# An attention and spiking-FFN kernel whose weighted sums, side work and transposes are put in other slots

## The reference

```
xn = layernorm(x)
q = einsum('bnhd,hed->bnhe', xn.reshape(B, N, 16, 16), Wq)
attn = softmax(einsum('bnhe,bmhe->bhnm', q, q) * 4)
s = einsum('bhnm,bmhe->bnhe', attn, q).reshape(B, N, D) @ Wp.T + bp
h = square(relu(xn @ W_fc.T))          # 1024 hidden
y = h @ W_proj.T
spikes = five steps: mem = 0.9*mem + y - reset; count mem > 1
out = x + s * silu(count / 5)
```

## Time and profile before

| what | value |
|---|---|
| median of 3 runs | 2579.01 us (2578.52 to 2580.41) |
| profiled execution, its own time | 2580.22 us |
| span of the profiled execution | 2578.3 us |
| mean granted TensorE clock | 0.991 of full speed |
| PE, ACT, DVE, POOL busy | 94%, 77%, 61%, 29% |

### The profile page before, as it was taken

How to read it: one execution, slowest core, us unless ns; L and a number is a source line. 1 busy time by engine, 2 the same in 40 slices (tenths; PEclk the granted TensorE clock), 3 DMA queues, 4 the chain that set the end, 5 groups by cost and what they waited for, 6 DMA issues and landing times.

```text
span 2578.3 us, 63759 instructions
## 1 busy us (share of the span) xinstructions
PE 2419.0 (94%) x23484; PEld 920.8 (36%) x23484; DVE 1567.1 (61%) x2581; ACT 1983.1 (77%) x2121; POOL 737.4 (29%) x681
## 2 busy tenths in 40 slices
PE   4999999999999999999999999999999999999997
PEld 2333333333333333333333333333333333333333
DVE  6456555766556675555765556665556755557664
ACT  2778778787777878778787787877778787787775
POOL 5123222333222332222332223332223332223420
PEclk7999999999999999999999999999999999999998
DMA  3011030210302102030110302102021120301200
GB/s 123 26 43 58 18 100 18 59 54 13 94 18 74 44 26 76 18 100 19 43 59 18 100 18 63 55 14 89 18 78 40 31 72 18 100 18 46 73 18 27
DMA packets 61487, 127.36 MB, mean 49 GB/s; under 512 B 15873, under 2 KB 17154, under 8 KB 58754
## 3 DMA queue, kind: packets, MB, share of 16 engines
q1 hardware_dynamic: 61186, 123.25, 15.5%
HBM read 89.11 MB, written 34.08 MB: 48 GB/s over the span
## 4 chain that ended last, share of the span: by engine, by line
PE 71%; ACT 14%; DVE 8%; issue 4%; SPq 1%; ACTq 0%; DMA 0%; DVEq 0%; POOL 0%; POOLq 0%
PE acc L624 34%; PE scores L650 18%; ACT e L804 14%; PE aux L541 8%; PE aux L550 7%; PE aux L532 2%; DVE cnt L931 2%; PE aux L598 1%; DVE r L913 1%; PE aux L556 1%; DVE h_t L919 1%; DVE acc_t L944 1%; SPq L447 1%; DVE q_hi L855 1%; DVE res L974 1%
## 5 line engine op out<-in xcount | busy, mean ns | idle before, releaser
L804 ACT ACTIVATE e<-scores 128x1024 f32<-128x1024 f32 x2048 | 1941.9, 1028 | 550.7 <-PE scores L650 550.5
L624 PE MATMUL acc<-e,v_ones 128*32 128x512 f32 x8192 | 986.6, 599 | 4.5 <-DVE acc_t L944 3.4
L650 PE MATMUL scores<-query_stack,key_stack 49*128 49x512 f16 x4096 | 712.6, 384 | 86.8 <-ACT e L804 59.4
L1176 POOL TENSOR_TENSOR r_squared<-r 128x512 f32<-128x512 f32 x256 | 266.5, 1041 | 996.2 <-DVE r L913 995.1
L541 PE MATMUL aux<-xn_t,w_fc 64*128 64x512 f16 x2976 | 454.7, 376 | 5.4 <-DVE xn_t L888 5.4
L550 PE MATMUL aux<-w_proj,h_t 64*128 64x256 f16 x6144 | 454.9, 270 | 1.3 <-DVE w_proj L901 1.3
L650 PEld LDWEIGHTS scores<-query_stack,key_stack 49*128 49x128 f16 x4096 | 158.9, 94 | 770.0 <-ACT e L804 726.7
L624 PEld LDWEIGHTS acc<-e,v_ones 128*32 128x32 f32 x8192 | 214.3, 109 | 464.6 <-issue 396.8
L550 PEld LDWEIGHTS aux<-w_proj,h_t 64*128 64x128 f16 x6144 | 334.8, 94 | 110.5 <-DVE w_proj L901 2.2
L1179 POOL TENSOR_TENSOR h_t<-r_squared,h_t 128x512 f16<-128x512 f32 x256 | 317.7, 1241 | 37.3 <-POOL r_squared L1176 1.7
L944 DVE STREAM_TRANSPOSE acc_t<-acc 128x512 f32<-128x512 f32 x128 | 91.2, 712 | 376.7 <-PE acc L624 376.7
(11 more groups left out here) (73 smaller groups left out, 980.3 us busy)
## 6 DMA issues: line engine op xcount, KB each, us to landing
key_stack<-q_scratch SPq DMA_DIRECT2D x384, 64.0 KB
query_stack<-q_scratch SPq DMA_DIRECT2D x384, 64.0 KB
x_tok<-x SPq DMA_DIRECT2D x16, 1024.0 KB, 5.0
x_out<-x SPq DMA_DIRECT2D x32, 512.0 KB, 3.7
out<-x_out SPq DMA_DIRECT2D x32, 512.0 KB, 2.7
q_scratch<-q_hi SPq DMA_DIRECT2D x32, 256.0 KB
q_scratch<-q_lo SPq DMA_DIRECT2D x32, 256.0 KB
query_stack<-c_scratch SPq DMA_DIRECT2D x128, 4.0 KB
```

The lines of the kernel that those rows point to most:

```text
L624: ins = nc.tensor.matmul(acc[STRIP * n:STRIP * (n + 1), :], v_ones[:, j, G * g + n, :], e[:, tile, n % 2, :], start=j == 0, stop=j == TT - 1)
L650: return nc.tensor.matmul(bank, key_stack[base:base + 49, at, j * P:(j + 1) * P], query_stack[base:base + 49, at, half * HALF:(half + 1) * ...
L804: nc.scalar.activation(e[:, tile % NE, :, :], scores[tile % 2][:, :, :], ACT.Exp, scale=4.0 if exact else SCORE_SCALE).then_inc(s.exp_done, 1)
L1176: nc.gpsimd.tensor_tensor(r_squared[:, :], tile, tile, ALU.mult).then_inc(s.rsq_set, 1)
```

## The change

Five things are changed together.

1. The weighted sums of a unit are no longer four blocks of two. At steps 0, 1, 3, 4 and 6 of each unit PE runs blocks of 1, 2, 1, 2 and 2 sums (BLOCKS). The steps with a block of one make one score tile, their side slot, and a second score tile.
2. Side work is shared over 64 slots, one for each step, with weights 3, 4, 4, 3, 4, 4, 4, 4 by the step's place in its unit (SHARE).
3. The four XT groups of the next batch move from the third stretch to the second (slots 18 to 21 of 64) and all use bank 0. Q groups come at slots 32, 34, 36 and 38, with banks 2, 0, 1 and 2; the C groups at slots 42 and 44, with banks 1 and 2.
4. The relu of the eight FC groups that are made ahead of the first batch runs on ScalarE (`relu_ahead`), and DVE splits the folded weight and W_proj between the groups.
5. The planned times of DVE, POOL and ScalarE tasks are set anew in steps.

```
-ROUNDS = STEPS // ROUND
-LAG = 2
+LAG = 4
+BLOCKS = {0: 1, 1: 2, 3: 1, 4: 2, 6: 2}
+SHARE = [3, 4, 4, 3, 4, 4, 4, 4]
-BANK = {FC: [k % KF % 3 for k in range(16)], Y: [1, 2, 1, 2], PROJ: [2, 0, 2, 0], XT: [2, 0, 1, 2], Q: [0, 1, 2, 0], C: [1, 1]}
+BANK = {FC: [k % KF % 3 for k in range(16)], Y: [1, 2, 1, 2], PROJ: [2, 0, 2, 0], XT: [0, 0, 0, 0], Q: [2, 0, 1, 2], C: [1, 2]}
-    return (0, 0, 9, 21, 32) if first else (0, 9, 15, 24, 30) if last else (0, 9, 16, 25, 32)
+    return (0, 0, 22, 46, 64) if first else (0, 15, 30, 45, 60) if last else (0, 15, 32, 50, 64)
...
-                    for n in range(ROUNDS):
-                        for i in range(ROUND * (n - LAG), ROUND * (n - LAG) + ROUND):
-                            if i >= 0:
-                                pv(b, i)
+                    for i in range(STEPS):
+                        for n in range(i - LAG, i - LAG + BLOCKS.get(i % TT, 0)):
+                            if n >= 0:
+                                pv(b, n)
                             elif not first:
-                                pv(b - 1, STEPS + i)
-                        score_tile(b, 4 * n)
-                        score_tile(b, 4 * n + 1)
-                        for piece in rounds[n][0]:
+                                pv(b - 1, STEPS + n)
+                        if i % TT in BLOCKS:
+                            score_tile(b, 2 * i)
+                            if BLOCKS[i % TT] == 2:
+                                score_tile(b, 2 * i + 1)
+                        for piece in slots[i]:
                             side(piece)
-                        score_tile(b, 4 * n + 2)
-                        for piece in rounds[n][1]:
-                            side(piece)
-                        score_tile(b, 4 * n + 3)
+                        if BLOCKS.get(i % TT) == 2:
+                            score_tile(b, 2 * i + 2)
+                        else:
+                            score_tile(b, 2 * i + 1)
...
+                def relu_ahead(k):
+                    act.wait_ge(s.pe_done[FC], k + 1)
+                    wait(act, s.h_set, k - 1)
+                    nc.scalar.activation(r[:, k % 2, :], aux[BANK[FC][k]][:, :], ACT.Relu, scale=HS ** 0.5 / (XS * WS)).then_inc(s.relu_set, 1)
...
-                        at = unit * TT // ROUND + TT // ROUND + LAG - 1 + 0.42
+                        at = TT * unit + TT + LAG - 1 + 0.42
```

More of the change, by code:

```diff
@@ L119, in streams @@
              [(0, FC, k) for k in range(8)] + [(-1, PROJ, 2)]]
[L120 to L123, removed]
-def slot_starts(begin, end, lengths):
[L128 to L132, removed]
+    second = [[(0, Y, 0), (0, FC, 8), (0, Y, 1)], [(-1, PROJ, 3), (0, Y, 1), (0, Y, 0)]]
@@ new lines, in streams @@
+    if first:
+        early = [[], []]
+        second = [[(0, Y, 0), (0, Y, 1), (0, FC, 8)], [(0, Y, 1), (0, Y, 0), None]]
+    return [(early, [12] * 9), (second, [48, 48, 12] if first else [60, 48]),
+            ([[(0, FC, k) for k in range(9, 16)] + [(0, PROJ, 0), (0, PROJ, 1)], [(0, FC, k) for k in range(8, 16)] + [(0, PROJ, 0)]], [12] * 9),
+            ([[(0, Y, 2), None if last else (1, FC, 0), (0, Y, 3)], [(0, PROJ, 1), (0, Y, 3), (0, Y, 2)]], [60, 48])]
+def slot_starts(begin, end, lengths):
+    share = [SHARE[i % TT] for i in range(begin, end)]
+    at, slot, starts = 0, begin, []
+    for n, length in enumerate(lengths):
+        goal = (at + length) / sum(lengths) * sum(share)
+        upto = slot + 1
+        while upto < end - (len(lengths) - n - 1) and sum(share[:upto - begin]) + SHARE[upto % TT] / 2 <= goal:
+            upto += 1
+        upto = end if n == len(lengths) - 1 else upto
+        own = share[slot - begin:upto - begin]
+        starts += [(at + length * sum(own[:i]) / sum(own), slot + i) for i in range(upto - slot)]
+        at, slot = at + length, upto
@@ L133, in slot_starts @@
     return starts
 def plan(first, last, exact):
-    rounds, ends = [[[], []] for _ in range(ROUNDS)], {}
+    slots, ends = [[] for _ in range(STEPS)], {}
     begins = stretches(first, last)
-    for n, pair in enumerate(streams(first, last)):
+    for n, (pair, lengths) in enumerate(streams(first, last)):
         if not pair[0]:
             continue
-        lengths = [60, 48] if n % 2 else [12] * 9
         starts = slot_starts(begins[n], begins[n + 1], lengths)
@@ L156, in plan @@
                     at += COLUMNS[kind]
-        opened = set() if n % 2 == 0 else {(-1, PROJ, 3), (0, PROJ, 1)}
-        if n % 2 == 0:
-            opened = {pair[1][0]}
+        opened = {pair[1][0]} if n != 1 or not first else set()
         for at, rows, group, i in sorted(pieces):
@@ L172, in plan @@
[L172 to L182, removed]
+                if i == PIECES[kind] - 1 and later:
+                    slots[slot].append(group + (None, 0, True, True))
+            else:
+                slots[slot].append(group + (rows, i, not later, later))
@@ new lines, in plan @@
+            if i == PIECES[kind] - 1 and later:
+                ends[group] = slot + 0.99
+        if last:
+            continue
+        whole = []
+        if n == 1:
+            whole = [(XT, k, (12 if first else 18) + k) for k in range(4)]
+        if n == 2:
+            at = [index for start, index in starts for half in range(9) if abs(start - 12 * half) < 1e-6]
+            whole = [(kind, k, at[half]) for half, (kind, k) in PLAIN.items()]
+        for kind, k, slot in whole:
+            if not (exact and kind == C):
+                slots[slot].append((1, kind, k, None, 0, True, True))
+                ends[(1, kind, k)] = slot + 0.98
@@ L183, in plan @@
     if exact:
-        for slots in rounds:
-            for pieces in slots:
-                pieces.sort(key=lambda piece: piece[2] if piece[1] == Y else 0)
+        for pieces in slots:
+            pieces.sort(key=lambda piece: piece[2] if piece[1] == Y else 0)
     ahead = [(0, FC, k) for k in range(KF)] if first else []
@@ L189, in plan @@
         ends[group] = -1.0 + 0.1 * group[2]
-    return ahead, rounds, ends
+    return ahead, slots, ends
 def placed(first, last, at):
@@ L689, in body @@
                 def body(b, parity, first, last):
-                    ahead, rounds, _ = plan(first, last, exact)
+                    ahead, slots, _ = plan(first, last, exact)
                     if exact:
@@ L1051, in run @@
                                                    ALU.mult, ALU.subtract).then_inc(wq_split, 1)
-                for kind, k in prep_groups(exact):
-                    bank = aux[BANK[kind][k]]
+                for n, (kind, k) in enumerate(prep_groups(exact)):
+                    bank = aux[prep_bank(n)]
                     if kind == XT and exact:
@@ L1077, in body @@
                         if kind == FC:
-                            tasks.append((at, relu, (b, k, bank)))
+                            tasks.append((at, relu, (b, k, bank, first and not exact and k < KF)))
                         if kind == Y and (last or k < 2):
```

100 lines of the change are left out of this document (52 added, 48 removed).

## The result

The changed kernel takes **2608.61 us** (2607.47 to 2610.23, 4 runs), the kernel before 2579.71 beside it (2578.52 to 2581.21, 4 runs): ratio 1.0113, 95% interval 1.0098 to 1.0128, so slower by 1.1%, 7.6 us beyond the forecast of 2601 and inside its range. The profiled execution after has a span of 2606.3 us, 28.0 more than before.

The account below looks back on a forecast made before the run. The prediction took PE as the bound, not the clock or DMA. Its terms, 28 - 6 - 30 + 36 - 6 = +22 us on the median of 2579.01, gave 2601 us, range 2564 to 2622.

Parts of the forecast that it names:

- D: New PE waits on DVE at XT, fourth Q, first C group and acc hand-overs: 2.6 us per middle batch, +36 us.
- A: One more block of sums per unit, 128 in all, each costing 0.22 us beyond its sums: +28 us, bounds 0 and +58.
- The Trainium skill's rule on mode changes: At blocks of sums, tiling changes drain TensorE; two drains per block would be 0.33 us, making the blocks' term 42 us.
- B: Score tiles' wait for ACT: 7.6 us per middle batch before, 7.2 after; -6 us over 15 batches, from -30 to 0.
- C: Three once-a-batch PE waits on DVE, at C, XT and FC groups, go with the new banks and places: -30 us.
- The lower bound of 0.6 per batch: Least size given for the new waits on DVE under D, each place at its least: +8 us in all.
- E: First batch: earlier weight splits start Y pieces at about 52, fewer bank waits, later XT input: -6 us, from -12 to 0.
- DVE is on time: Rival: places under D wait at most 0.6 us per batch, 2564 to 2573 us; faster cases together had 0.24.
- DVE becomes the bound at the hand-overs: Rival: half of eight acc hand-overs wait 0.3 to 1.1 us, 2643 us; above 2620, with dearer blocks, had 0.13.

Follow-up runs that it names:

- experiment 5: The changed kernel with only the table of blocks altered to one sum in every block, uneven side-work shares kept: 2570.90 us, ratio 0.9962 to the kernel before.
- experiment 1: The changed kernel with four blocks of two sums per unit again, take_sums and place_v one slot earlier: 2606.24 us, ratio 1.0102 to the kernel before.
- experiment 3: The changed kernel with one sum in every block and even shares of side work: 2570.78 us, ratio 0.9962 to the kernel before.
- experiment 7: The kernel before with each round's two sums apart, one ahead of each pair of score tiles, take_sums and place_v later: 2604.73 us, ratio 1.0094.
- experiment 8: The changed kernel with one sum in every block, even side-work shares and two spike tasks one slot later: 2535.28 us, ratio 0.9825 to the kernel before.
- experiment 2: The changed kernel with two spike tasks of the third stretch planned one slot later: 2599.12 us, ratio 1.0077 to the kernel before.

## Why the prediction was right

The direction and the main mechanism held: the change removes about 30 us of waits on DVE, brings in more of others, and pays for its blocks. One term, D, was 10 us too low and another, A, some 6 too high, so the errors cancelled in part.

- **A, the blocks, +28: a little too large.** The block of one takes 1.00 us as foretold, and 2 x 1.00 - 1.86 = 0.14 is entry and exit. The tile ahead takes 0.31. But in a light round the slots between single tiles take 0.65 where I had 0.69, and twice that is about what the tile adds. So the 0.22 is 0.13 in light rounds and 0.24 in full ones (experiment 5), 17 to 31 us for 128 blocks. The estimate from experiment 1 is 22.
- **The Trainium skill's rule on mode changes** (TensorEngine Tiling (Array Packing), Key Properties), by which, with 166 ns for a drain, the term was to be 42 us: entry and exit together take 0.14 us here, less than half of the 0.33 for two drains, so that estimate is not borne out.
- **B, the wait for ACT, -6: the number came near, the place was wrong.** The list goes from 59.4 to 67.8 us, but all gaps together from 78.5 to 78.3. In a middle batch the trace has 23 gaps ahead of score tiles before and 19 after, as the plan counted. They sum to 4.3 and 4.6 us; with the 0.12 that each takes beyond its gap this is an estimate of 7.1 and 6.9 us, near the 7.6 and 7.2 of the plan. So a middle batch gains 0.2, some 3 us in all. The first batch gains 6 from the blocks: it takes 138.9 us with them, 144.9 without (experiment 1). The reason given, that only steps with two sums can wait, is borne out by experiments 3, 5, 7 and 8, where no two sums stand together and 1.1 to 3.0 us of the wait are left in the whole kernel.
- **C, -30: right.** All three waits are gone.
- **D, +36: right in kind, 10 too low.** The listed waits are 25.8 (Q), 12.0 (C), 7.2 (XT) and 4.8 less the 3.4 of before (`acc`), 46.4 us. In a middle batch they are 1.6, 0.9, 0.4 and 0.4, where the forecast had 1.0, 0.7, 0.5 and 0.4: the fourth Q group is the miss. From the end of the unit's last sum at 1084.50 DVE takes 10.6 us to the end of `h_t` (10.2 to 11.0 foretold) and PE 8.9 to the group's place (9.2 foretold). No wait held PE up on the way, which the 1.0 had counted on; the 1.8 had not. That two spike operations in DVE's queue carry most of the wait is shown by experiment 2; that such a wait moves to `acc` when it is removed was not foreseen. The lower bound of 0.6 per batch was not each place at its least either: 0.5, 0.3, 0.1 and 0 are 0.9.
- **E, the first batch, -6: right in size, half of its reasons.** The first sum starts 3.0 us earlier. The first batch takes 138.9 us instead of 145.3, but 144.9 with the blocks undone, so the fewer banks to wait for gave next to nothing and the rest belongs to B. The first Y piece starts at 54.19, not at 52: the last `h_t` ends at 54.09. Without a term, 1.4 us more are saved from the start of the last batch to the end.

With these sizes the sum is about 22 - 9 - 30 + 46 - 4 = +25 us, against 28.0 measured in the span. It can't close better: A is an estimate, the listed waits hold those of the first batch too, and that batch's 6 us are already net of its blocks. One middle batch closes: 0.9 of busy time, 0.3 of gaps ahead of the score tiles (4.6 less 4.3) and 1.5 of other waits (3.5 less 2.0) are its 2.75 us. Fourteen of them are 38.5, and the start, the first and the last batch take 3.0, 6.4 and 1.4 off.

Of the rivals, "DVE is on time" and "DVE becomes the bound at the hand-overs" both fell: the places under D waited 3.3 us per batch, not 0.6, and the hand-overs 4.8 us in all, not 42. That second mechanism is real all the same, since experiment 7 shows it at 41.9 us.

## What to carry to other kernels

Where two engines pass tiles through two buffers, a long stretch without tiles and a close run of them behind it make the first engine wait. Splitting the stretch costs 0.13 to 0.24 us here and frees 0.45 where little other work stands between the tiles, but only 0.28 where much does, so it pays in light rounds and breaks even in full ones. Splitting one block of four took only 4 of 23 waits away and cost 0.5 us per middle batch; splitting all took every one. Two views of one wait can disagree: the list that leaves out short gaps showed 8 us more where the whole idle time had not changed. Where another engine's queue is dense, a wait that leaves one place is looked for at the next hand-over before it is counted as a gain. The worth of an edit depends on the others: these two took 37.8 and 9.5 us alone and 73.3 together, so parts of a reordering are tried in pairs as well.

## What the runs showed of the hardware

**The granted clock can fall behind a short wait.** In experiment 5 the batch of 157.60 us does the same work as that of 156.29. The wait of its fourth Q group, and three windows around the end of it (busy times as above, then the granted clock):

```profile
1075.50 1.22 PE L547 MATMUL aux<-xn_t,w_q 128*128 128x512 f16 x3 [1.98 <-DVE h_t L945]
...
1074.00:1076.00 2.00, 0.50 (x2) 0.21 (x3) 1.34 (x3) 0.00 (x0) 1.13 (x2) 0.95 0.00 0
1076.00:1078.00 2.00, 2.00 (x8) 0.30 (x10) 1.21 (x2) 0.69 (x1) 1.53 (x2) 0.50 0.00 0
1078.00:1080.00 2.00, 2.00 (x18) 0.42 (x10) 1.93 (x4) 0.71 (x2) 0.57 (x1) 0.70 0.10 22
```

After a wait of 1.98 us the granted clock is 0.50, the lower of the two levels (1.2 GHz), until about 1079, and the three matmuls of the Q group take 1.22 us where they take 0.82 in the batch before. That batch has the same wait of 1.98 us (ending at 919.43) and keeps the clock at 1.00. The drop costs 1.3 us per batch where it comes, two thirds of the wait. Counted over the 14 middle batches, the clock falls at this place in 7 of experiment 5 and in 11 of experiment 3, all with a wait of 1.98; in none of the changed kernel, with a wait of 1.60; and in none of experiment 8, where the wait is 0.57 and the batches take 154.3 to 154.6. What decides between two batches with the same wait no run shows.

**A spike count of 1.53 us instead of 0.69** stands beside POOL's work. In experiment 8:

```profile
1062.58 1.16 POOL L1208 TENSOR_TENSOR h_t<-r_squared,h_t 128x512 f16<-128x512 f32 x1
1062.75 1.53 DVE L957 SCALAR_TENSOR_TENSOR cnt<-y_sb,cnt 128x512 f32<-128x512 f32 x1
```

The count begins 0.17 us after POOL and ends 0.54 after it; the excess of 0.84 is less than the 0.99 for which both run, and 1062.75 + 1.53 - 0.69 = 1063.59 lies near the end of POOL's at 1063.74. So it looks as if DVE waits for most of POOL's operation. The Trainium skill (SBUF — State Buffer, Terms) says that DVE and GpSimd take turns on a shared pair of ports, held for a whole instruction; the row agrees but for 0.15 us, by which the count ends earlier than 0.69 after POOL's end. No run here took POOL's work away, but the trace of the kernel before has both cases: of its 256 counts on L931, the 89 that no POOL operation overlaps all take 0.69 us, and the 167 that one overlaps take 0.88 to 1.55. The `h_t` operation on L919, which reads one of its two inputs from PSUM, takes 0.69 in all its 241 overlaps. The length of DVE's queue ahead of a wait depends on this by 0.8 us per operation. It also moved with the change: the counts of that line take 281.6 us in all before and 214.0 after, more than the 59.6 us by which DVE is busy less.
